# A two-layer graph kernel on one core: idle products on TensorE in both layers, and GpSimd's gathers of the first layer wait only for the slot and the indices

## The reference

```python
def _L0_gnn_ref(x, edge_index, edge_attr, timestamps, We1, be1, We2, be2, Wt, bt, Wn1, bn1, Wn2, bn2):
    ef = jax.nn.relu(edge_attr @ We1 + be1) @ We2 + be2
    tw = jax.nn.sigmoid(timestamps[:, None] @ Wt + bt)
    ef = ef * tw
    combined = jnp.concatenate([x[row], ef], axis=1)
    msg = jax.nn.relu(combined @ Wn1 + bn1) @ Wn2 + bn2
    return jax.ops.segment_sum(msg, col, num_segments=x.shape[0]) + x

def _L1_gnn_ref(x, edge_index, W1, b1, W2, b2):
    h = x + jax.ops.segment_sum(x[src], dst, num_segments=x.shape[0])
    h = jax.nn.relu(h @ W1 + b1) @ W2 + b2
    return jax.nn.relu(h)

edge_index = jnp.stack([src, dst])
h = jnp.maximum(_layernorm(x), 0.0)
x = x + _L0_gnn_ref(h, edge_index, edge_attr_64, edge_weight, ...)
h = jnp.maximum(_layernorm(x), 0.0)
x = x + _L1_gnn_ref(h, edge_index, ...)
```

## Time and profile before

| | before |
|---|---|
| median of 3 runs (lowest to highest) | 3646.17 us (3644.92 to 3647.67) |
| span of the profiled execution | 3603.9 us |
| what lies around the span, as median less span | 42.3 us |
| mean granted TensorE clock, 1 being full | 0.804 |
| TensorE, VectorE, GpSimd busy | 74%, 54%, 58% of the span |
| first layer's pairs (with windows), about | 150 to 2580 us of the span |
| second layer's pairs, about | 2676 to 3545 us of the span |

### The profile page before, as it was taken

One profiled execution on the slowest core, in us unless ns is written; L12 is line 12 of the kernel. 1 busy time (PEld: TensorE's weight loads), 2 busy tenths in 40 slices (PEclk: granted clock), 3 DMA queues, 4 the chain that ended last, 5 costly groups with the idle time before them and its releaser, 6 DMA issues.

```text
span 3603.9 us, 51709 instructions
## 1 busy us (share of the span) xinstructions
PE 2652.8 (74%) x14584; PEld 1610.3 (45%) x14585; DVE 1962.6 (54%) x4063; ACT 1009.1 (28%) x1000; POOL 2098.5 (58%) x2125
## 2 busy tenths in 40 slices
PE   4687788877877778778877788785645766766766
PEld 3344444444444444444444444343332545544544
DVE  8665566655656566656655566665673333233333
ACT  3233333333333333333333333232231111111112
POOL 6566666666666666666666665555254555555552
PEclk8788888888888888878888888887875777877777
DMA  6444444444433343444344343333122434334332
GB/s 196 113 127 134 127 127 136 125 130 128 126 121 125 123 124 122 123 125 124 120 122 128 120 128 115 120 117 96 32 101 83 132 118 129 122 95 128 101 114 61
DMA packets 229418, 426.82 MB, mean 118 GB/s; under 512 B 82703, under 2 KB 141584, under 8 KB 229072
## 3 DMA queue, kind: packets, MB, share of 16 engines
q0 software_dynamic: 74752, 153.23, 16.3%
q1 hardware_dynamic: 103152, 177.42, 15.0%
q10 hardware_dynamic: 51266, 93.34, 7.4%
HBM read 364.35 MB, written 59.43 MB: 118 GB/s over the span
## 4 chain that ended last, share of the span: by engine, by line
PE 39%; issue 20%; DVE 17%; another core or an unknown queue 12%; DVEq 10%; SPq 1%; DMA 1%; ACT 0%; POOL 0%; ACTq 0%
PE ps L925 9%; PE ps L836 8%; PE ps L795 8%; DVE nodes L1185 5%; PE ps L804 5%; PE ps L815 4%; PE ps L787 3%; DVEq L1119 3%; DVEq L1165 2%; DVE hot L1140 2%; DVE acc L1127 1%; DVE arena L1185 1%; DVEq L1182 1%; PE ps L915 1%
## 5 line engine op out<-in xcount | busy, mean ns | idle before, releaser
L537 POOL DMA_INDIRECT big<-table,idx x2080 | 2032.9, 977 | 1375.8 <-issue 587.6
L836 PE MATMUL ps<-nodes 128*128 128x500 bf16 x1280 | 448.5, 469 | 335.8 <-DVE nodes L1185 180.3
L795 PE MATMUL ps<-arena,we 128*128 128x512 f32 x784 | 511.9, 784 | 29.7 <-issue 12.2
L640 ACT ACTIVATE big<-big 128x1024 f32<-128x1024 f32 x196 | 207.2, 1057 | 1074.3 <-DVE big L1134 917.5
L815 PE MATMUL ps<-hot,big 128*128 128x64 f32 x3136 | 395.9, 275 | 112.8 <-issue 86.0
L1185 DVE TENSOR_SCALAR nodes<-iota_k,win_off,nodes 128x500 bf16<-128x500 f16 x1280 | 453.7, 407 | 0.0
L815 PEld LDWEIGHTS ps<-hot,big 128*128 128x128 f32 x3136 | 381.6, 195 | 107.0 <-issue 104.6
L1182 DVE TENSOR_TENSOR nodes<-iota_b,nodes 128x384 bf16<-128x384 f16 (+1 forms) x492 | 245.4, 499 | 266.8 <-remote 174.8
L1134 DVE TENSOR_TENSOR big<-ps,big 128x1024 f32<-128x1024 f32 x196 | 239.3, 1221 | 244.2 <-issue 242.6
L836 PEld LDWEIGHTS ps<-nodes 128*128 128x128 bf16 x1280 | 106.3, 106 | 573.6 <-DVE nodes L1185 271.1
L630 ACT ACTIVATE arena<-ps,cols 128x1024 f32<-128x1024 f32 x196 | 218.5, 1115 | 418.7 <-PE ps L787 229.2
(11 more groups left out here) (147 smaller groups left out, 2534.2 us busy)
## 6 DMA issues: line engine op xcount, KB each, us to landing
arena<-in_ew SPq DMA_DIRECT2D x196, 512.0 KB
arena<-in_ea SPq DMA_DIRECT2D x196, 256.0 KB
counts_d<-arena ACTq DMA_DIRECT2D x192, 245.0 KB
acc<-counts_d ACTq DMA_DIRECT2D x15, 2940.0 KB
big<-table,idx POOLq DMA_INDIRECT x2080
table<-big SPq DMA_DIRECT2D x7, 672.0 KB, 3.0
idx<-in_src SPq DMA_DIRECT2D x260, 4.0 KB
xs<-in_x SPq DMA_DIRECT2D x7, 448.0 KB, 5.5
```

What stands on the lines that cost most here:

```text
L537: pool.indirect_dma_start(to(u, q, t), None, table, bass.IndirectOffsetOnAxis(ap=idx[:, u, at:at + 1], axis=0))\
L795: pe.matmul(p_ef[q], we2[:, :], hid[:, q, :], start=True, stop=True).then_inc(ef_mm, 1)
L836: m = pe.matmul(to, hots[:, t, :], keys[:, t, :], start=False, stop=True, skip_group_check=True)
```

## The change

Three things. (1) In the first layer, in front of the hidden products of each pair but the first, TensorE runs four products of 128x128 by 128x500 (fp16) whose result is overwritten; they stand behind the wait for `hid_made` and ahead of the wait for `ea_loaded`. (2) In the second layer TensorE runs three such products ahead of the waits of `sum_rows` and three behind it, into a bank that the layer does not use. (3) All bodies of the first layer gather with `free`: the waits for `ef_mm` and `agg_mm` are gone.

```diff
+FILL0 = 4
+FILL1 = 3
...
+        p_idle = ps[:, 5 * BANK:5 * BANK + CK]
...
             for b in range(1, NBODY):
-                gather_body(b, b >= NBODY - 2)
+                gather_body(b, True)
...
+            def idle_products(to, count):
+
+                for _ in range(count):
+                    pe.matmul(to, iota_b[:, :], iota_k[:, :], start=True, stop=True, skip_group_check=True)
+
             def hidden_products(b, u, n, first):
-                pe.wait_ge(ea_loaded[u], b * 16 + 16)
                 if not first:
                     pe.wait_ge(hid_made, n)
+                    idle_products(p_hid[0][:, 0:CK], FILL0)
+                pe.wait_ge(ea_loaded[u], b * 16 + 16)
                 for q in (0, 1):
...
                 n = b * (2 * RING) + 2 * u
+                idle_products(p_idle, FILL1)
                 pe.wait_ge(hot1_made, n + 2)
                 for q in (0, 1):
...
                 i.then_inc(slot1_free, 1)
+                idle_products(p_idle, FILL1)
```

## The result

The changed kernel takes 4016.45 us (median of 4 runs, 4004.45 to 4049.72), the kernel before 3646.92 us (4 runs, 3644.92 to 3652.77): a ratio of 1.101 [1.097, 1.106], 370 us more. The prediction had the sign and not the size: 3810 us, with a range that ended at 3930. One execution of one experiment (e11, 3915.00 us, the one that its trace shows) counts as slow, being over 1.5% above the fastest of its kernel, and is left out of its ratio.

What follows compares the result with a forecast made beforehand. Bound: a round of waits, no engine full, TensorE held back while GpSimd gathers without pause. Free gathers +94, first layer's idle products +46, second layer's +24: +164 on 3646.2, 3810 us; own range 3660 to 3930, 8 in 10 3400 to 3930.

Steps and rivals of the forecast that it cites:

- The signs that were named: Changed kernel's profile: waits moved to VectorE's messages, issue stalls after 10 us of gathering, 13 us or more per first-layer pair.
- The price by GpSimd's pace: First layer's free gathers: 13.22 us per pair, 0.51 more than 12.71, over 184 pairs: +94 us.
- The other bound of that step: First layer's free gathers priced by TensorE's steps: 7.7 us per body over 46 bodies, +354 us.
- the second layer, +24: Second layer's six idle products per pair: +51 us less 27 credited for the clock; bounds -47 and +191.
- the first layer's idle products, +46: Four idle products per first-layer pair: +96 us less 50 credited for the clock; bounds nothing and +382.
- all hidden: First layer's idle products: lower bound, their time vanishes in waits that follow, costing nothing.
- The step of one in four: First-layer step where TensorE's own pace ends the wait; four idle products at half clock, 48 x 1.99 = +96 us.
- The rival of the clock: Idle products hold TensorE's clock in both layers, making the kernel faster: 3540 us, 3520 to 3640; chance 0.12.
- The rival of the floor: First layer's free gathers run at GpSimd's floor, 10.2 us per pair: faster, 3300 to 3560 us; chance 0.26.
- The base of the sum: Whole kernel's starting time: profiled span 3603.9 us plus 42.3 around it, set to meet the median, 3646.2 us.

Runs made afterwards that it cites:

- e11: Kernel before with free gathers; only slots 0 and 2 wait for the previous pair's landing, so 16 gathers stand between breaks: 3885.80 us, 1.063.
- e5: Kernel before with free gathers in the first layer, each pair first waiting until the previous pair's gathers have landed: 3505.72 us, 0.973.
- e10: Changed kernel, all three edits, with each first-layer pair waiting until the previous pair's gathers have landed: 3574.59 us, 0.979 against the kernel before.
- e1: Kernel before with the free gathers alone (waits for ef_mm and agg_mm removed), no idle products: 3908.30 us, 1.085.
- e3: Kernel before with only the second layer's six idle products per pair, gathers with both waits: 3623.47 us, 1.006.
- e12: Kernel before with free gathers, landing breaks per pair in the first layer and for slots 1 to 3 in the second, no idle products: 3497.53 us, 0.959.
- e2: Kernel before with only the first layer's four idle products, gathers with both waits: 3601.32 us, 1.000.
- e4: Changed kernel without the second layer's idle products (free gathers and the first layer's four): 3939.13 us, 1.093 against the kernel before.
- e15: e12 with the first layer's four idle products added, on the fifth chip: 3388.69 us, 1.184 against the kernel before.
- e8: Kernel before with only the wait for ef_mm removed, agg_mm kept: 3563.17 us, 0.990.
- e7: Kernel before with only the wait for agg_mm removed, ef_mm kept: 3773.67 us, 1.048.

## Why the prediction was off

**Right: where it would go wrong.** The mechanism was stated as a guess, "while GpSimd gathers without a pause, TensorE's signals and its own issue are held back, and a pause lets them go". e5 and e10 bear it out by putting a pause of another kind into each pair; e11 by making the gapless stretch long again. What the prediction didn't see is that the kernel before has these stretches to the same extent (288 us beyond 10 us on end in 2000, beside 289), so it took the removed waits for the pauses that keep the stall away. The signs that were named came: GpSimd's waits left TensorE's lines for VectorE's messages (L1147, where L1145 was named), at 6.5 us each (4 to 5 were given); "issue" stalls in the products behind some 10 us of gathering; more than 13 us per pair; idle products at 408 ns each on the mean, between the two levels of the earlier trace rows. The clock of the second layer, given as some 0.75, came at 0.80.

**Wrong: the step "The price by GpSimd's pace ... 0.51 more than 12.71 ... +94 us".** The edit costs 305.5 us on the first chip and 335 on the fifth group's. By the windows it is 14.22 - 12.71 = 1.51 us per pair, three times the 0.51. The pace was taken from 24 gathers of the earlier trace rows, which begin behind a pause of 15.23 us (the first row there) and hold two short ones, 4.93 and 3.81 us. The long pause of a round was left out of the price; counted in full it would have given 18.2 us per pair, so this stretch, which is no whole round, could not be priced either way. (Nor was it quite gapless: the second gather comes 1.69 us after the first has ended, so only 15 of the 16 gathers stand on end, from 2473.81, and the stall of the earlier trace rows some 10 us behind that.) In the changed kernel the 577.7 us of GpSimd's waits fall on 34 bodies (1097 gathers, 32 each), 16.9 us per body, twice the 8.7 that I counted. The other bound of that step, by TensorE's steps of the earlier trace rows, 7.7 us per body and +354, came close, in part by luck: it too covered slots 1 to 3 alone, and over all four slots a body of e1 is 6.0 us longer (4 x 1.51). The reason given against it ("it counts the work done and not one engine's place in it") holds only for a stretch that is a whole round. In the body after, slots 1 to 3 take 41.90 us where the free one of the earlier trace rows took 37.30.

**Right size: the second layer, +24.** e3: +20.7 us. The changed kernel's second layer loses 52 us by its pace, and e10, with the six products and no break there, takes 77 us more than e12; these are larger, and why the term grows in that company was not tried.

**Wrong by itself, near in company: the first layer's idle products, +46.** Alone nothing (e2, -1.5 us, its bound "all hidden"); on top of the free gathers +30.8 (e4). The step of one in four that I charged in full is not on the path of the kernel before: the wait that ends there lets GpSimd go, and it goes at the same pace all the same (1258 gathers against 1259). In sum, 164 were predicted and 357 measured on the chip of the parts: 211 too little for the free gathers, 18 too much for the rest.

**The rival of the clock falls as a rival of time.** The idle products did raise the clock: 0.84 to 0.87 (e2) and 0.73 to 0.83 (e3), and in the changed kernel 0.80 in the second layer. The Trainium skill's rule ("TensorE: Matmul & The Clock Gate", The HAM clock gate), that the throttled state is the default and activity lifts it, is borne out by these rows. The time didn't follow: 1.000 and 1.006. TensorE's products weren't what the round waited for.

**The rival of the floor** is what the fifth chip shows, 10.19 us per pair, but there for the kernel before already. The changed kernel and e1 were not run on it, so whether the change is neutral there was not tried.

**The base of the sum.** 3603.9 + 42.3 was set to meet the median. In the changed kernel's profiled execution the time is 4012.79 us for a span of 4011.0, so 1.8 us lie around it. The profiled execution of the kernel before was then some 40 us faster than the median, such as two of the experiments' chips give (3602.78 and 3601.52); on which chip it ran is not on record. It changes no term.

## What to carry to other kernels

A wait that looks like a needless coupling may decide when an issuing engine pauses, and so where another engine is held up; before removing it, look in the trace for a stretch that already runs without it, and price it over a whole round of the waits, from one long pause to the next, never between two short ones. Where a stall follows long gapless gathering, a break of one landing (2.5 us) after each eight gathers was worth 10 to 11% against none, and one after each four cost as much as it gave. Measure the kernel before on the same chip each time. Kernels with breaks gained 2.7 to 4.1% on chips with the hold; kernels with breaks lost 4 to 18% on the one without, among them e15 (18%), which is the fastest kernel of the others, e12, with four idle products. No kernel with a break ran on both.

## What the runs showed of the hardware

- While GpSimd issues indirect gathers of 128 rows each 1.25 us without a break, TensorE begins after some 10 us to get its products out one or two at a time, with 0.3 to 1.5 us ahead, and VectorE waits up to 16.7 us for a signal. In the changed kernel TensorE's idle share "issue" is 3% up to 10 us of gathering, 57% from 10 to 15 us and 67% beyond. A break of 2.5 us in every pair keeps nearly all of it away (e5).
- This was so on four chips of the experiments (3601.52 to 3649.37 us for the kernel before), and absent on a fifth (2861.29 us), where 1256 gathers ran with 0.3 us between them and TensorE had no wait "issue" in 1600 us. One program, 21% apart. Each chip was met in one group only, so that it was a state of the hour and not the chip is not excluded.
- The cost doesn't follow the amount of such gathering: 387 us beyond 10 us on end in 2000 us went with 0.990 of the time (e8), 312 us with 1.048 (e7).
- What is held (the fetching of TensorE's instructions, its semaphore signals, or something that both share with the descriptors of the gathers) the runs don't tell; nor whether the break works by GpSimd's silence or by the landing. That stays open: the kernels made for it met the chip without the hold. The DMA packets that the profile marks "instruction" are at least not long under way: from 400 to 2400 us none took over 1.7 us in the changed kernel, nor over 1.6 in the kernel before.
- Raising the clock from 0.73 to 0.83 by idle products in the second layer came with 5% fewer gathers in the same time, on another chip, and with 20.7 us more: a higher granted clock is no gain in itself.
